# A four-matmul quad sum whose first term is copied into the PSUM bank by ScalarE

## The reference, cut to what matters

```python
w_m = (efeat @ W_msg + b_msg).reshape(E, in_f, -1)
w_a = (efeat @ W_attn + b_attn).reshape(E, in_f, -1)
h_src = feat[src][:, :, None]
e1 = w_m * h_src
e2 = w_a * h_src
seg_max = jax.ops.segment_max(e2, dst, num_segments=N)
ex = jnp.exp(e2 - seg_max[dst])
denom = jax.ops.segment_sum(ex, dst, num_segments=N)
attn = ex / denom[dst]
ft = jax.ops.segment_sum(e1 * attn, dst, num_segments=N)
return ft.sum(axis=1)
```

## Time and profile before

| | |
|---|---|
| median of three runs | 8912.76 us (8904.54 to 8920.91) |
| the profiled execution's own time | 8910.58 us |
| its span, first to last instruction | 8908.9 us |
| PE busy over the span | 7159.9 us (80%) |
| DVE busy | 7506.5 us (84%) |
| ACT busy | 4804.9 us (54%) |
| POOL busy | 6381.3 us (72%) |
| mean granted TensorE clock | 0.897 |

### The profile page before, as it was taken

The page is one execution under the profiler, slowest core; times in us unless marked ns, Lnnn a source line. Parts: engine busy times, 40 slices in busy tenths (PEclk is TensorE's granted clock), DMA queues, the critical chain, the costliest instruction groups (busy, mean ns, idle before and its releaser), DMA issues. The chain is left out here.

```text
span 8908.9 us, 135582 instructions
## 1 busy us (share of the span) xinstructions
PE 7159.9 (80%) x35152; PEld 4074.4 (46%) x35152; DVE 7506.5 (84%) x11807; ACT 4804.9 (54%) x7730; POOL 6381.3 (72%) x6335
## 2 busy tenths in 40 slices
PE   3888857888887088888888889488888888888884
PEld 3776744565565055555555555233333333333331
DVE  7999956788888388888888888499999999999997
ACT  5999956666775065665666556233333333333333
POOL 6777767777776677777777777377777777777774
PEclk9989967888888589999999999699999999999997
DMA  4222211111111111111111111122222222222223
GB/s 155 64 62 63 62 42 45 45 46 46 48 46 43 15 29 31 28 33 28 33 28 28 33 28 18 20 72 76 76 76 80 78 76 76 76 76 78 81 76 100
DMA packets 499695, 493.19 MB, mean 55 GB/s; under 512 B 181075, under 2 KB 396906, under 8 KB 498731
## 3 DMA queue, kind: packets, MB, share of 16 engines
q1 hardware_dynamic: 299595, 371.60, 12.4%
q0 software_dynamic: 199904, 119.78, 8.1%
HBM read 240.96 MB, written 249.95 MB: 55 GB/s over the span
## 5 line engine op out<-in xcount | busy, mean ns | idle before, releaser
L2524 POOL DMA_INDIRECT attn_got<-tab,attn_line x1760 | 1912.2, 1086 | 791.6 <-issue 503.5
L1982 POOL DMA_INDIRECT sheaf_got<-tab,sheaf_idx x1612 | 1702.7, 1056 | 488.5 <-issue 470.2
L2577 PE MATMUL attn_q<-attn_X,ident 128*128 128x512 f32 x3520 | 1718.0, 627 | 101.5 <-ACT attn_S L2657 92.5
L2071 PE MATMUL sheaf_acc<-sheaf_hot_hi,sheaf_wide 128*128 128x392 bf16 x6696 | 1355.1, 345 | 283.3 <-DVE sheaf_hot_hi L2274 281.5
L1508 POOL DMA_INDIRECT nnconv_got<-tab,nnconv_idx x1116 | 1081.4, 969 | 381.9 <-issue 321.6
L2577 PEld LDWEIGHTS attn_q<-attn_X,ident 128*128 128x128 f32 x3520 | 652.1, 198 | 1193.5 <-issue 1193.5
L2714 DVE TENSOR_TENSOR attn_T<-attn_w,attn_got 128x1024 f32<-128x1024 f32 x880 | 1052.8, 1217 | 152.0 <-PE attn_w L2568 116.7
L2657 ACT COPY attn_S<-attn_q 128x512 f32<-128x512 f32 x440 | 255.9, 582 | 1531.2 <-PE attn_q L2584 1531.2
L1173 POOL DMA_INDIRECT gcn_got<-tab,gcn_idx x868 | 827.6, 953 | 304.0 <-issue 277.1
L2071 PEld LDWEIGHTS sheaf_acc<-sheaf_hot_hi,sheaf_wide 128*128 128x128 bf16 x6696 | 655.8, 106 | 819.7 <-issue 491.1
L1267 PE MATMUL gcn_acc<-gcn_hot,pieces 128*128 128x512 f32 x2604 | 740.6, 442 | 196.7 <-ACT gcn_hot L1321 134.1
(11 more groups left out here) (508 smaller groups left out, 13676.9 us busy)
## 6 DMA issues: line engine op xcount, KB each, us to landing
sums<-attn_S SPq DMA_DIRECT2D x110, 1024.0 KB, 5.1
tops<-attn_S SPq DMA_DIRECT2D x110, 512.0 KB, 2.9
attn_got<-tab,attn_line POOLq DMA_INDIRECT x1760
sheaf_got<-tab,sheaf_idx POOLq DMA_INDIRECT x1612
gcn_key<-src_key SPq DMA_DIRECT2D x62, 384.0 KB
gcn_blk<-src_blk SPq DMA_DIRECT2D x62, 384.0 KB
nnconv_got<-tab,nnconv_idx POOLq DMA_INDIRECT x1116
nnconv_key<-src_key SPq DMA_DIRECT2D x62, 256.0 KB
```

Of the source, the lines that this page charges most:

```text
L1982: e.indirect_dma_start(out=got[at.b][:, j, D:D + T2], out_offset=None, in_=tab[2], in_offset=indices(idx[at.b], j)).then_inc(s_got[half][a ...
L2071: mm = e.matmul(pacc[k][:, 0:HH], wide[at.b][half][:, part, col, :], hot[:, k * HH:(k + 1) * HH], start=False, stop=False, skip_group_chec ...
L2524: e.indirect_dma_start(out=got[at.b][:, 4 * q + n, :], out_offset=None, in_=tab[3], in_offset=indices(ids[:, q, n, :], D + 2)).then_inc(s_ ...
L2577: e.matmul(to, ident[:, :], X[:, q, :, n, :], start=n == 0, stop=False)
```

## The change

ACT gets a new function `begin_sum(at, q)`. It waits for the products of the quad (`s_prod`) and for the last state copy (`s_state`), copies `X[:, q, :, 0, :]` into the bank `pq` and adds one to the new semaphore `s_begun`. PE's quad sum waits for `s_begun` in place of the two old semaphores, and issues only the products `n = 1, 2, 3` and the carry, all with `start=False`, so that they add onto what ACT wrote. Ahead of the stage's first work PE issues one matmul into `pq` with `start=True`, which opens the bank for adding; ACT waits for it (`s_open`) before anything else in the stage.

```diff
+            s_begun, s_open = seml("begun", "open")
...
                     e.wait_ge(s_w, 16 * 5 * (P // RW))
+                    e.matmul(pq[:, :], ident[:, :], Wc[:, :], start=True, stop=True).then_inc(s_open, 1)
...
-                        turn_wait(e, s_prod, at.of(QB, q + 1))
-                        turn_wait(e, s_state, at.of(QB, q + 2))
-                        for n in range(4):
-                            e.matmul(to, ident[:, :], X[:, q, :, n, :], start=n == 0, stop=False)
+                        turn_wait(e, s_begun, at.of(QB, q + 1))
+                        for n in range(1, 4):
+                            e.matmul(to, ident[:, :], X[:, q, :, n, :], start=False, stop=False, skip_group_check=True)
                             if between and n == 2:
                                 between()
...
-                        e.matmul(pq[:, :], passes[at.b][:, q, :], before, start=False, stop=True).then_inc(s_quad, 1)
+                        e.matmul(pq[:, :], passes[at.b][:, q, :], before, start=False, stop=False,
+                                 skip_group_check=True).then_inc(s_quad, 1)
...
                     e.sem_inc(s_state, 2)
+                    e.wait_ge(s_open, 1)
...
+                    def begin_sum(at, q):
+
+                        e.wait_ge(s_prod, at.of(QB, q + 1))
+                        if q > 0 or at.k > 0:
+                            e.wait_ge(s_state, at.of(QB, q + 2))
+                        e.copy(pq.rearrange("p (t c) -> p t c", t=2), X[:, q, :, 0, :]).then_inc(s_begun, 1)
...
                             put_state(prev, 1)
+                            begin_sum(prev, 2)
                             put_state(prev, 2)
+                            begin_sum(prev, 3)
...
                             passing(at.plus(1))
+                        begin_sum(at, 0)
                         put_state(at, 0)
+                        begin_sum(at, 1)
...
                         put_state(At(NBQ - 1), q)
+                        if q < QB - 1:
+                            begin_sum(At(NBQ - 1), q + 1)
```

## The result

The changed kernel takes 9297.81 us (median of four runs, 9289.47 to 9310.27), the kernel before 8916.42 us in the same comparison. The ratio is 1.0432, with a 95% interval of 1.042 to 1.0445: 4.3% slower. The forecast was 9300. The profiled execution took 9304.59 us, 394.0 us more than the 8910.58 of before; its span is 9302.9 us.

What follows compares the result with a forecast made beforehand. The prediction took a chain over DVE, PE and ACT, with no engine full, as the bound: 108 blocks x (30.8 - 27.32) = 376, plus 14 for the start, on 8910.6 gives 9300 us; range 9000 to 9350.

Steps and rivals of the forecast that it cites:

- The ring: Chain over DVE, PE and ACT setting each attention block's length: 27.32 us mean before, 30.8 us forecast after the change.
- The price of the half clock: PE's longer idle before quad 0 drops its clock to half, adding 2.7 us a block; bounds nothing and 4.77.
- The ring at full clock: Attention block's chain with the change and PE at 2.4 GHz: 28.1 us, 0.8 above the 27.32 mean.
- quad 0's stretch with `matrices`: On PE: two products, `matrices(k+2, 0)`, the last product and the carry, 4.77 us at full clock.
- the state and the copy: On ACT between PE's quads 0 and 1: state copy, new copy and handover to PE, 1.38 us.
- Rival 1: Same longer chain in the attention block, but PE's clock stays at 2.4 GHz: 9009 us, chance 0.14.
- Rival 2: PE rules the attention block; ACT reaches quad 0's copy early enough, so faster or level: 8899 or 8878 us, chance 0.06.
- Rival 3: Half clock lasts through quad 1's sum on PE: another 1.8 us a block, 9490 us, chance 0.05.
- Rival 4: ACT's writes to the bank are dropped or overwritten by adding matmuls; same time as the forecast, sharing its 0.70 chance.
- The start: Stage's opening: ACT waits for PE's opening matmul and its weights, delaying POOL's first gathers, 14 us.
- The end of the stage: Each of the last three sums gains 0.86 - 0.62 us; nothing much.
- The size of a copy: ACT's 512-column copy from SBUF into PSUM: 0.59 us, kept between 0.40 and 0.75.

Runs made afterwards that it cites:

- late start alone: Kernel before, all four products on PE and no copy, with quad 0's sum also waiting until passing(k+1) on ACT is done: 9288.15 us, ratio 1.0419.
- quad 0 on PE: Changed kernel with quad 0 summed by four PE products, ACT copies only for quads 1 to 3, no opening matmul or wait for it: 8910.73 us, ratio 0.9996.
- early copy: Changed kernel with begin_sum(k, 0) moved up on ACT from behind passing(k+1) to behind weights(k, 2): 8928.36 us, ratio 1.0015.
- clock kept up: Changed kernel plus six unread matmuls a block in PE's idle times, three after quad 3's sum and three after matrices(k+1, 3): 9044.8 us, ratio 1.0146.

## Why the prediction was right

**The ring and what it gives up.** The working named the ring through DVE, PE and ACT, the copy of quad 0 behind `passing` as what enters it, and PE's start at 17.1 us of it. The trace after has 7024.05 - 7006.97 = 17.08. The run with the late start alone has the same loss with no copy in it, the run with quad 0 on PE and the one with the early copy have nearly none of it with three or four copies. So the cause is the place of one instruction on ACT, and not the copies or the adding onto ACT's data.

**The price of the half clock** was put at 2.7 us a block, between the rows with 2 us and 8 us of idle time. It measured 2.3: 30.72 less the 28.4 of the run with the clock kept up. The ring at full clock was put at 28.1 (its terms add up to 28.16) and measured 28.4. The parts of the difference are small: in the run with the clock kept up PE's start is 17.17, quad 0's stretch with `matrices` 4.94 where I had 4.77 (7021.72 - 7016.78), the state and the copy 1.47 where I had 1.38. The two errors cancel to 0.1, so that the block of 30.8 was met at 30.72 better than either term deserved. The rows show where the 2.3 lie: the four records of quad 0 take 3.68 us in place of 1.89, and `matrices` 1.60 in place of 1.07 (7029.33 - 7027.73 against 7019.74 - 7018.67 in the run with the clock kept up). The price is what the half clock meets in the ring and no constant: with the late start alone it meets six records, 4.54 us in place of 2.58, which is 2.0.

**Rival 1** (the clock stays up) would have been the case of the run with the added matmuls, 9044.8 against its 9009. **Rival 2** (PE rules the ring, the change is level or faster) is what the early copy makes of the change: its condition, PE's start before 15.75 us, holds there (14.09), and the time is level. Where between 14.1 and 17.1 us the loss sets in wasn't tried. Its own price, 0.24 us a block faster, was right only with the clock kept up (27.07 to 26.88); without, the longer idle time after quad 3 took it back. The prediction had named that idle time but not applied it to this rival. **Rival 3** (half clock through quad 1) didn't happen: its six records take 2.81 us after the 1.44 us pause. **Rival 4** (ACT's data lost) has the forecast's own time, and no time tells it from the forecast; it is out because the sums hold the term that ACT wrote (last section).

**The start** was put at 14 us: 14.2 in the trace. **The end of the stage** was put at nothing, and that step was wrong: it costs 8.8 us. I had counted only the last three sums, which gain 0.2 us each. In the last block quad 0's sum starts 13.7 us after `drop` where it was 6.4 us, as its copy stands behind the exponentials, `tops_out` and state 3 (`passing` has no next block there), and it then runs at half clock (5.46 us for six records). That this was hidden in the total is luck: 376 + 14 forecast, 365 + 14 + 9 measured, 390 and 388.

**The size of a copy.** ACT's copy from SBUF into the bank takes 0.587 us in the mean of 421, its copy out of the bank 0.581. The rule of the Trainium skill ("ScalarE: Activation LUTs", "Step-by-step: what each stage is for") that ScalarE reaches PSUM faster than SBUF doesn't show in the durations here: the copy with PSUM as its destination isn't the shorter one, though the two also differ in where they read. The row taken for it, 0.59, was right.

## What to carry to other kernels

Before work is moved to an idle engine, ask where on that engine's stream the new instruction stands, not how busy the engine is: ACT was busy 36% of the stage, and one 0.6 us copy at the end of its block's work cost 370 us, while the same copy six instructions earlier left the block as long as before. What is gained by taking work off TensorE can be lost again to its clock, where it then idles longer; a run whose idle time is filled by matmuls that nobody reads tells the two apart. Here the copies for quads 1 to 3 gained next to nothing alone (8915.45 to 8910.73 us); the filling gained 24.5 us in the kernel before (8912.67 to 8888.17), and on top of it the copies gained as much again (8863.6).

## What the runs showed of the hardware

- Matmuls with `start=False` add onto what ACT wrote into the bank, once a matmul with `start=True` has written the bank: one such matmul ahead of the stage serves its 440 sums, and with quad 0 on PE the `start=True` of that quad serves the three sums after it. No run leaves the opening matmul out.
- Different kernels had nearly the same block with half clock in it: 30.72 us for the change and for the late start alone, although the granted clock of the stage was 0.83 in the one and 0.89 in the other, and 27.32 us before, 27.31 with quad 0 on PE and 27.30 with the early copy, at 0.96, 0.94 and 0.90. The rings at full clock differ (28.4 and, by the working, 28.7; 27.07, 26.87 and 26.88). What holds the lengths together wasn't tried.
- In the kernel before, with 1.98 us of idle time after quad 3, the clock fell to half 69 times in the some 102 blocks between 5900 and 8700 us; with quad 0 on PE, where PE idles 3.28 us there, it fell 102 times, once in each block.
